# A hybrid SSM / DeltaNet / FFN block on one core: two small statistics tiles allocated behind the activation tiles instead of ahead of them

## The reference, cut to what matters

```
x = x + ssm(layernorm(x))          # gated state-space layer, 8 heads, rotary state, W_in, W_out
x = x + ffn(layernorm(x))
x = x + deltanet(layernorm(x))     # delta-rule attention, 8 heads of 32, Wq, Wk, Wv, Wb
x = x + ffn(layernorm(x))
ffn(x): h = silu(x@w1.T*s1) * (x@w2.T*s2)        # 256 -> 1024
        h = gelu(h@h1.T*sh1); h = gelu(h@h2.T*sh2)   # 1024 -> 1024, twice
        return h@w3.T*s3                          # 1024 -> 256
```

## The kernel before, in words

| tile (line) | first byte | modulo 256 |
|---|---|---|
| w1_sb, w2_sb, h1_sb, h2_sb, w3_sb (L181 to L185) | 16544, 24736, 32928, 65696, 98464 | 160 each |
| x_sb (L215) | 133344 | 224 |
| in_mv, in_ve, drstd (L224 to L226) | 146016, 146048, 146080 | 96, 128, 160 |
| in_mv0, drstd0 (L227, L228) | 146112, 146144 | 192, 224 |
| xf_hi, xf_lo (L230, L231) | 146176, 148224 | 0 |
| hA_hi, hA_lo, hB_hi, hB_lo (L232 to L235) | 150272, 158464, 166656, 174848 | 0 |
| hid, gate, xnf (L236 to L238) | 183040, 187136, 189184 | 0 |
| first tile of the attention stages (xn, xnd) | 191232 | 0 |

## Time and profile before

### The profile page before, as it was taken

How to read it: one execution, slowest core, us unless ns; L and a number is a source line. 1 busy time by engine, 2 the same in 40 slices (tenths; PEclk the granted TensorE clock), 3 DMA queues, 4 the chain that set the end, 5 groups by cost and what they waited for, 6 DMA issues and landing times.

```text
span 2538.7 us, 61583 instructions
## 1 busy us (share of the span) xinstructions
PE 2285.3 (90%) x25057; PEld 2045.2 (81%) x25088; DVE 1355.8 (53%) x3346; ACT 1106.2 (44%) x2153; POOL 844.6 (33%) x1001
## 2 busy tenths in 40 slices
PE   5799986978998999988999989999899899999898
PEld 4688965867887888877888878878788787987788
DVE  4655154665545664465645566456563655546531
ACT  3465331643335633365333643347333473333233
POOL 3223331323333333333333333333333333333233
PEclk8799997988999999999999999999999999999999
DMA  8000000000100001000010000100010000000000
GB/s 253 1 1 1 1 18 18 2 1 18 30 7 1 2 19 33 4 1 2 18 35 2 1 5 16 35 2 2 8 31 17 1 1 18 22 7 18 18 10 9
DMA packets 85468, 43.84 MB, mean 17 GB/s; under 512 B 69936, under 2 KB 80048, under 8 KB 85168
## 3 DMA queue, kind: packets, MB, share of 16 engines
q1 hardware_dynamic: 81504, 28.11, 4.5%
q0 software_dynamic: 3664, 11.53, 1.4%
HBM read 27.05 MB, written 12.58 MB: 16 GB/s over the span
## 4 chain that ended last, share of the span: by engine, by line
PE 66%; DVE 15%; issue 7%; POOL 6%; ACT 4%; DMA 1%; SPq 0%; DVEq 0%; POOLq 0%; ACTq 0%
PE F L1317 29%; PE F L1297 6%; PE Q L1376 5%; PE F L1339 4%; POOL hA_lo L604 3%; PE Q L1477 2%; PE Q L1450 2%; PE Q L1433 2%; DVE hid L963 2%; PE Q L1545 2%; PE Q L1410 2%; PE Q L1388 1%; PE Q L1364 1%; PE Q L1557 1%; PE Q L1414 1%
## 5 line engine op out<-in xcount | busy, mean ns | idle before, releaser
L604 POOL TENSOR_TENSOR hA_lo<-hid,hA_hi 128x256 fp32r<-128x256 f32 (+1 forms) x384 | 361.4, 943 | 690.4 <-DVE hA_hi L967 346.4
L1317 PE MATMUL F<-hB_hi,h_sb 128*128 128x256 f32 x2048 | 512.1, 290 | 3.3 <-POOL hB_lo L604 2.7
L1317 PE MATMUL F<-hA_hi,h_sb 128*128 128x256 f32 x2048 | 509.6, 288 | 3.4 <-DVEq L966 2.4
L1317 PE MATMUL F<-hB_lo,h_sb 128*128 128x256 f32 x2048 | 499.1, 282 | 0.0
L1317 PE MATMUL F<-hA_lo,h_sb 128*128 128x256 f32 x2048 | 496.9, 282 | 0.0
L1317 PEld LDWEIGHTS F<-hB_hi,h_sb 128*128 128x128 f32 x2048 | 387.0, 189 | 14.2 <-POOL hB_lo L604 6.8
L1317 PEld LDWEIGHTS F<-hA_hi,h_sb 128*128 128x128 f32 x2048 | 386.1, 189 | 13.1 <-POOL hA_lo L604 5.2
L1317 PEld LDWEIGHTS F<-hB_lo,h_sb 128*128 128x128 f32 x2048 | 388.5, 190 | 0.0
L1317 PEld LDWEIGHTS F<-hA_lo,h_sb 128*128 128x128 f32 x2048 | 386.6, 189 | 0.3
L1297 PE MATMUL F<-xf_hi,w_sb 128*128 128x256 f32 x1024 | 282.8, 309 | 42.3 <-DVEq L966 32.6
L732 ACT ACTIVATE hid<-F,sh_sb 128x256 f32<-128x256 f32 x256 | 121.5, 475 | 425.4 <-PE F L1317 424.7
(11 more groups left out here) (198 smaller groups left out, 4124.6 us busy)
## 6 DMA issues: line engine op xcount, KB each, us to landing
h_sb<-h_dram POOLq DMA_DIRECT2D x2, 4096.0 KB, 23.9
x_sb<-x_dram SPq DMA_DIRECT2D x8, 512.0 KB, 4.2
a_scr<-amv SPq DMA_DIRECT2D x32, 128.0 KB, 2.3
au<-a_scr SPq DMA_DIRECT2D x8, 512.0 KB, 3.2
t_scr<-ti SPq DMA_DIRECT2D x8, 512.0 KB, 2.6
tbd<-t_scr SPq DMA_DIRECT2D x128, 32.0 KB, 1.9
out_dram<-x_sb SPq DMA_DIRECT2D x8, 512.0 KB, 3.0
w_sb<-w_dram POOLq DMA_DIRECT2D x3, 1024.0 KB, 7.9
```

What stands on the lines that cost most here:

```text
L604: pool.tensor_tensor(lo, hid[:, n % 2, 0:w, :], hi.bitcast(F32), ALU.subtract).then_inc(f_lo.handle, 1)
L1317: last = pe.matmul(ps[:, i * TOK:(i + 1) * TOK], w[:, k, o:o + P], part[:, k, :], start=(i == 0 and k == 0 and part is src[0]), stop=(i == ...
```

## The change

The two allocation lines of `in_mv0` and `drstd0` move from ahead of `xf_hi` to behind `xnf`. They take 32 bytes each (drstd0 has 16, rounded up), so every tile between the old and the new place stands 64 bytes lower: `xf_hi`, `xf_lo`, `hA_hi`, `hA_lo`, `hB_hi`, `hB_lo`, `hid`, `gate` and `xnf` go from a remainder of 0 to 192 modulo 256 (0 to 64 modulo 128, 0 to 0 modulo 64). `in_mv0` and `drstd0` come to stand at 191168 and 191200. All else stays where it was: `x_sb` and the weights are allocated ahead of both places, the attention tiles behind both. No instruction, wait or DMA is added, removed or put elsewhere in its stream.

```diff
         in_mv = sb("in_mv", [P, NT, 2])
         in_ve = sb("in_ve", [P, NT])
         drstd = sb("drstd", [P, NT])
-        in_mv0 = sb("in_mv0", [P, NT, 2])
-        drstd0 = sb("drstd0", [P, NT])
 
         xf_hi = sb("xf_hi", [P, 2, 2, P], F32R)
         xf_lo = sb("xf_lo", [P, 2, 2, P], F32R)
...
         hid = sb("hid", [P, 2, 2, TOK])
         gate = sb("gate", [P, 2, TOK])
         xnf = sb("xnf", [P, 2, D])
+        in_mv0 = sb("in_mv0", [P, NT, 2])
+        drstd0 = sb("drstd0", [P, NT])
```

## The result

| | before | after |
|---|---|---|
| median of 8 executions each | 2546.49 us | 2524.31 us |
| lowest and highest | 2542.66, 2555.73 us | 2520.80, 2535.51 us |
| profiled execution, its own time | 2540.47 us | 2528.67 us |
| its span | 2538.7 us | 2526.9 us |

The two profiled executions show only 11.8 us of it, because that of before was shorter than all eight executions of its kernel in the table, and that of after was the second longest of its eight.

The account below looks back on a forecast made before the run. PE, busy for 90% of the span and 66% of the chain, was taken to bound the kernel. All terms summed to 0, so the forecast stayed at the median, 2546 us, with a range of 2530 to 2562.

Parts of the forecast that it names:

- What bounds the kernel: PE bounds it, 66% of the chain; 8250 matmuls of L1317, L1297, L1339 there, 8.25 us per nanosecond each.
- Instructions, statistics tiles, ACT, DVE, POOL at 0: Everything outside PE: no instruction changes, moved tiles cost the same; 0, bounds 0.2, 0.9, 0.7 and 0.7 us.
- PE at 0: Matmuls of L1317, L1297, L1339 on moved tiles keep their pace; taken as 0, bounded by 14.0 us either way.
- my three reasons: For 0 on PE: remainders modulo 64 stay, 120.0 ns holds while blocks change, other engines show no address effect.
- The bound of 1.7 ns: L1317's 120.0 against L1339's 118.3 ns per matmul, taken as PE's limit both ways: 14.0 us.
- Rule and row: Skill pages against PE's trace: estimated 109.2 ns per matmul, two independent read ports, so no address could matter.
- the 10.8 ns: Each PE matmul's excess over the page's figure; 89 us less if a removed read collision, given no chance of its own.
- Rival A: PE stream distance modulo 128: L1317 and L1297 go to 118.3 ns, L1339 to 120.0; 11 us less, chance 0.11.
- Rival S: PE streams nearer modulo 256, 32 bytes instead of 96, get in each other's way; 41 us more, chance 0.10.
- Rival N: The change does less than it says: `x_sb` doesn't move; time as forecast, no case of its own.
- The chance of 0.79 for no effect: Whole kernel: chance given to the moved tiles' addresses changing nothing, time staying within about 0.5% or 12.7 us.

Follow-up runs that it names:

- e9_both_192: Kernel before with pads changed so the moving operand starts 192 bytes past the stationary one, modulo 256, in L1317, L1297 and L1339; median 2514.36 us, ratio 0.9864.
- e1_weights_64: Kernel before with the FFN weights 64 bytes further back modulo 256, activations in their old place; median 2521.24 us, ratio 0.9894.

## Why the prediction was wrong, point by point

*What bounds the kernel* held. One nanosecond per matmul was worth 8.25 us on the end, and that exchange rate gives the result: on the chain of before, L1317 has 29% (736 us, 6140 matmuls at 0.1199 us), L1297 6% (152 us, 1270) and L1339 4% (102 us, 860). With the paces measured that is 6140 x 2.9 + 1270 x 2.1 - 860 x 0.2 = 20.3 us less, against 22.2 in the medians. In e9_both_192 the same sum is 6140 x 5.4 + 1270 x 3.3 + 860 x 3.0 = 39.9 us, against 34.6 measured (0.0136 x 2546): there the chain has begun to move to DVE.

*Instructions, statistics tiles, ACT, DVE, POOL at 0* held: no duration followed the tiles' place (the two DVE groups that changed did so with the tiles unmoved as well), and the run that moved the weights alone had the whole gain.

*PE at 0* is the step that failed. I had the two streams of unlike pace before me, 120.0 and 118.3 ns for one shape, bounded the effect by their difference, and took 0 inside it. What the runs showed in its place is 2.9 ns less on L1317 and 2.1 less on L1297, by the distance of the two operands alone. None of my three reasons held. That every start keeps its remainder modulo 64 decides nothing: D 0, 64, 128 and 192, all 0 modulo 64, have 119.7, 117.0, 118.7 and 114.5 ns. That the 120.0 ns hold while the blocks change by 512 to 8192 bytes (by the kernel's loops some steps are larger, and all are multiples of 512) fits any period that divides those steps, and one of 256 does. And what ACT, DVE and POOL show does not carry over to PE, whose two operands are read by two instructions that overlap (PE busy for 90% of the span, PEld for 81%). The bound of 1.7 ns was too narrow because two places on an unknown curve don't bound it.

*Rule and row.* The Trainium skill, TensorE: Matmul & The Clock Gate, section Back-to-back issue gap, would give an estimated 109.2 ns by its formula for a single gap, and no run here came to that; the best steady pace in a long stretch was 113.3 ns. As to the Trainium skill, SBUF — State Buffer, section Who interferes with whom, the runs contradict nothing that it says of other engines, but the pace of PE's stream hangs on where its two operands stand to each other: 114.5 to 119.9 ns by D alone. I saw the 10.8 ns that no rule covered and gave them no chance. Up to 6.7 of them (120.0 less 113.3) are what D takes or gives.

*Rival A* had the right kind of cause, the distance between the streams, and a wrong form of it, so that it had L1317 going faster by luck. Its period of 128 bytes made the two lines swap paces; L1317 went past L1339's 118.3 to 117.0, and L1339 stayed at 118.2 instead of going to 120. Its price, 11 us, was half of what came. *Rival S* had the period of 256 right and the sign wrong; nearness isn't what costs. *Rival N:* `x_sb` did not move, and it didn't matter.

The chance of 0.79 for no effect rested on a trace in which each line had been run at one D only. Such a trace can't show a dependence inside a line, and the one it does show, the 1.7 ns between L1317 at D 96 and L1339 at D 160, I set aside.

**What stays open.** That the two reads of PE collide in SBUF is an argument from the distances, not shown: no run took one of the reads away. Why the paces have these values, why a stretch falls into 113.4 or 117.8 ns at the same D, and how hi and lo share the cost, is open. That the period is no longer than 256 bytes rests on few comparisons: e1_weights_64 and the changed kernel differ by 256 bytes in their real distance (117536 and 117280 from h1_sb to hA_hi) and agree within 0.2 ns in L1317 and in L1339, and so do L1317 and L1339 at D 128, which lie 256 apart modulo 512. That it is no shorter rests on D 0 against 128 and 96 against 224. D was tried in steps of 32 bytes and once at 16.

## What to carry to other kernels

Where PE streams one float32r matmul of 256 columns after the other, each with its own weight load, look at the distance from start to start and compare lines of one shape; if they differ, the place of the moving tile against the stationary one, modulo 256, is a thing to scan, with a pad tile of 32 bytes and more ahead of the weights. Each padding tried here cost 256 bytes of SBUF per partition more than the kernel before (512 with `hA_lo` apart), and one profiled execution each seems enough for a first look: two layouts with the same D agreed within 0.2 ns in pace, twice, where single times of one kernel scatter by some 0.4%. As the share of the steady paces can differ from layout to layout, time the best ones again. Judge such a change by moving one operand, the other, and both.

## What the runs showed of the hardware that I had not expected

- The pace of one and the same matmul runs from 114.5 to 119.9 ns on average (4.5%) with nothing changed but the distance of two tiles, and with the clock fully granted over every long stretch compared (0.998 or more).
- At one D a stretch of 60 to 150 matmuls keeps one of at most two paces: 120.0 alone at D 96; 116.7 and 117.8 at D 32; 113.4 and 117.8 at D 192. The two halves of such a stretch differ by 0.65 ns at most.
- Two moving tiles at unlike D, read in turn, are slower than the mean of the two paces: 119.3 ns on average at 192 and 96, where 114.5 and 119.9 alone would give 117.2, and 117.5 at 192 and 64, where 114.5 and 117.0 would give 115.8.
